# A two-layer transformer block on one core: the second attention's local products with its exponentials as moving columns

## Chip, cores and metric

One core of one Trainium2 chip runs the whole program in one launch, in float32. The time is device microseconds (us), from 3 executions of the kernel. The engines are TensorE (PE, with its weight loads as PEld), VectorE (DVE), ScalarE (ACT), GpSimd (POOL) and SyncE (SP), each with its own instruction stream in a fixed order; they wait for one another by semaphores.

## What is computed

Eight sequences of 512 tokens and 128 features go through two layers. Each layer is an attention (a recurrence in the first, the one below in the second) and a mixture of eight experts of which each token takes two; both with layer norm and modulation around them. The change touches the second attention and the last sum.

```python
# second attention, per sequence x (512 x 128), 16 heads of 8
w = x.reshape(nW=8, 64, 16, 8)                       # windows of 64 tokens
attn = softmax(einsum('nqhd,nkhd->nhqk', w, w) * scale)
local = einsum('nhqk,nkhd->nqhd', attn, w).reshape(512, 128)
comp = conv1d(x, conv_w, stride=4)[:64] + conv_b      # 64 compressed keys
gt = concat([comp, global_memory])                    # 128 keys
glob = softmax(x . gt * scale) . gt                   # 16 heads
mix = sigmoid(concat([local, glob]) @ gate_w + gate_b)
y = (mix * local + (1 - mix) * glob) @ out_w + out_b
# last line of the second layer, y1 and y2 the token's two experts' weighted rows
out = x + gb * (y1 + y2)
```

## The kernel before

The program has four stages: the recurrent attention with the shared expert (0 to 386 us of the trace), the first experts (to 514 us), the second attention (to 1040 us), the second experts (to 1297 us); and then a last sum with loads and stores.

**The second attention** works on eight sequences of 512 tokens in ten steps, `step(i)` for i = -2 to 7, followed by `tail(7)`. Each engine has its own `step`, a list of calls written out by hand, and these lists are the order of the work. In step i each engine does parts of several sequences: f = i+2 (first norm, its sums and transposes), a = i+1 (compressed keys, maxima of the global scores), i itself (exponentials and products), b = i-1 (end of the local part, gate, output, residual), c = i-2 (second norm, modulation), d = i-3 (router, ranks, placing, scatter to the experts' rows in DRAM).

Scores come in six units, each of four PSUM banks (0 to 3) of 128 x 512: four for the global part (heads r of each of four groups g) and two for the local part (`score_local`, `again_local`, l = 0 and 1, four windows each). Every unit's scores are computed twice. In the first pass (`score_global` L2137, `score_local` L2149) DVE takes maxima (`max_global` L1036, `max_local` L1043); they are turned by TensorE (`max_T_global` L2159, `max_T_local` L2167) and negated by ACT. In the second pass (`again_global` L2185 with `less_global` L2194; `again_local` L2213 and L2209) the negated maxima are added, and ACT takes the exponentials (`exps`, L1702 and L1704) into `expT`, two buffers of four rows of 512. A bank can be filled again when the DVE has its maxima or ACT its exponentials (`bank_free` and the waits on c_exp).

**Global products** (`attend_global`, L2224): values of 128 keys x 32 columns are the stationary operand, exponentials move as 512 columns, and the four groups g write four different bands of 32 partitions. The sums stand in banks 6 (heads 0, 1) and 7 (heads 2, 3); ACT (`global_sums`) and DVE (`take_global`, L1058, L1059) take the lower and the upper half of each 32 partitions. `norm_global` inverts the sums (L1049), shuffles and multiplies.

**Local products** (`attend_local`, L2247): the exponentials of one pair of heads are the stationary operand (128 keys x 128), written by `exps` in a permuted order (`expT_l`), and 34 columns of values move: for each of the two windows in a tile 16 values and a one, whose column gives the sum. There are four calls in a step, (l, t) = (0,0), (0,1), (1,0) and, in the following step, (1,1); each has 8 products. The output has queries as partitions. `norm_local` (L1069, L1073) inverts 16 sums and multiplies two halves, per call. `turn_out` (L2261) turns the result back by 4 products, twice a step, and ACT's `mixed_T` (L1712) writes it into `lgT`, in two pieces of two.

After it come `gate` (L2277, L2278), `gate_tanh`, `difference` (POOL, L1371), `mix`, `out` (L1800), `residual` (L1089 and the norm's sums L615, L619), POOL's `ln_scale` and `normalise` (L1202, L1223), `modulate` (L1098, L1100), `h2_T`, `route` (L1805), `router`, `rank` (L1812, L1813), `place`, and POOL's `scatter` (L1234: 8 indirect DMAs a sequence). In `tail` stand what is left of sequence 5 (router, place, scatter), of 6 and of 7, with products that only keep TensorE busy (L1790).

**The last sum.** SP waits until the experts' rows are in DRAM (`y`), loads them, 512 KB a sequence (L599, packets of 1 KB), and stores the outputs (L602). DVE does for each sequence three operations on 128 x 512 (L820, L822, L824): y1 + y2, times gb, plus x.

A matmul or transposition of float32 stands in the trace as two instructions, each with its own weight load; the program order has one.

## Time and profile before

| | us |
|---|---|
| median of 3 runs | 1323.47 (1320.85 to 1325.7) |
| the profiled execution, its own time | 1323.05 |
| its span, first to last instruction | 1321.2 |
| mean granted clock of TensorE over the span | 0.921 of full speed |
| TensorE busy (matmul) | 1157.1, 88% |
| TensorE busy (weight loads) | 816.0, 62% |
| DVE busy | 820.8, 62% |
| POOL busy | 605.6, 46% |
| ACT busy | 497.1, 38% |
| chain that ended last: PE, issue, DVE, DMA, POOL | 58%, 11%, 9%, 8%, 7% |

The page's busy times are unions over overlapping instructions, and a matmul that waits inside a group can be counted as busy, since ends are modelled: for what a group takes, the distance from its start to the next group's start is read. "Granted clock" is 1.00 at 2.4 GHz and 0.50 at 1.2 GHz.

### The profile page before, as it was taken

What the parts mean: (1) busy time and instruction counts of PE and PEld (TensorE: products, weight loads), DVE (VectorE), ACT (ScalarE), POOL (GpSimd) and SP (SyncE); (2) the same over time, 40 slices, a digit from 0 to 9 for tenths busy, and PEclk for the clock granted to TensorE, in tenths of its full rate; (3) what the DMA queues carried; (4) which work ended last, traced back from release to release, by engine and by line L of the source; (5) the groups of instructions that cost most, each with busy time, mean ns of one, the idle gap of its engine ahead of it and who ended that gap; (6) DMA issues with size and microseconds to landing.
All of it is one profiled execution on the core that took longest, in us unless ns stands there. A gap on an engine that the chain in (4) does not pass through costs nothing.

```text
span 1321.2 us, 23979 instructions
## 1 busy us (share of the span) xinstructions
PE 1157.1 (88%) x8027; PEld 816.0 (62%) x8027; DVE 820.8 (62%) x2275; ACT 497.1 (38%) x1147; POOL 605.6 (46%) x706
## 2 busy tenths in 40 slices
PE   6868869867788889899999999999998899999990
PEld 3545546555358886346556465475554599999990
DVE  4678868887334444445457687766646366666665
ACT  3324434433314442142434444424331145444440
POOL 1556858887525554512224546532246233333330
PEclk9788989998889999998889999969899899999996
DMA  4976697673134522100101012000011341111106
GB/s 135 258 185 160 165 260 176 155 164 80 35 76 115 153 80 69 60 23 24 47 10 57 26 49 73 25 23 18 22 39 41 76 118 42 38 46 37 44 20 198
DMA packets 96530, 113.07 MB, mean 86 GB/s; under 512 B 11225, under 2 KB 81177, under 8 KB 93833
## 3 DMA queue, kind: packets, MB, share of 16 engines
q1 hardware_dynamic: 87512, 93.17, 27.1%
q0 software_dynamic: 8640, 17.84, 4.2%
q8 instruction: 66, 1.08, 0.3%
q10 hardware_dynamic: 256, 0.53, 0.2%
q14 instruction: 56, 0.45, 0.1%
HBM read 81.06 MB, written 32.04 MB: 86 GB/s over the span
## 4 chain that ended last, share of the span: by engine, by line
PE 58%; issue 11%; DVE 9%; DMA 8%; POOL 7%; ACT 3%; SPq 2%; DVEq 0%; ACTq 0%; POOLq 0%
PE bank L2027 8%; PE bank L2038 8%; PE bank L2247 5%; PE bank L2185 4%; PE bank L2137 4%; PE bank L2054 3%; PE bank L2194 3%; PE bank L2149 3%; PE bank L2224 3%; PE bank L2213 2%; POOL slots L1234 2%; DMA mrow<-mods 2%; DMA region<-vrdram 2%; POOL region L1270 2%; PE bank L2209 2%
## 5 line engine op out<-in xcount | busy, mean ns | idle before, releaser
L2027 PE MATMUL bank<-rows,wup 128*128 128x128 f32 x1136 | 154.7, 280 | 17.4 <-DVE wup L763 14.1
L1234 POOL DMA_INDIRECT slots<-pay,slot x128 | 130.0, 1016 | 83.4 <-issue 71.6
L1249 POOL DMA_INDIRECT y<-region,xin x78 | 83.9, 1075 | 154.0 <-ACT region L1614 140.7
L2027 PEld LDWEIGHTS bank<-rows,wup 128*128 128x128 f32 x1136 | 141.0, 195 | 21.3 <-DVE rows L751 10.4
L2038 PE MATMUL bank<-rows,wse 128*128 128x128 f32 x1136 | 141.9, 278 | 2.7 <-DVE wse L768 2.7
L2038 PEld LDWEIGHTS bank<-rows,wse 128*128 128x128 f32 x1136 | 132.2, 192 | 9.1 <-issue 7.9
L1036 DVE TENSOR_REDUCE rows<-bank 128x4 f32<-128x512 f32 x128 | 79.5, 684 | 92.6 <-PE bank L2137 86.7
L1249 POOL DMA_INDIRECT y<-hh,region x64 | 69.2, 1082 | 92.9 <-ACT hh L1614 81.9
L1702 ACT ACTIVATE w0uv<-bank 128x512 f32<-128x512 f32 x128 | 66.1, 602 | 90.5 <-PE bank L2194 90.4
L756 DVE SCALAR_TENSOR_TENSOR rows<-bank,bcol,rows 128x128 f32<-128x128 f32 x142 | 43.4, 346 | 90.8 <-ACT rows L1603 90.5
L1790 PE MATMUL bank<-consts 128*128 128x512 f32 x192 | 92.2, 627 | 0.0
L1270 POOL TENSOR_TENSOR region<-region 128x512 f32<-128x512 f32 x64 | 83.4, 1317 | 18.5 <-DVE region L917 17.5
L751 DVE TENSOR_TENSOR rows<-region,bank 128x256 f32<-128x256 f32 x71 | 29.9, 421 | 85.7 <-ACT region L1593 66.7
L1878 PE MATMUL bank<-consts,region 128*128 128x128 f32 x512 | 75.3, 302 | 5.9 <-POOL region L1270 5.7
L2247 PEld LDWEIGHTS bank<-region,w0uv 128*128 128x128 f32 x512 | 72.6, 225 | 11.3 <-issue 10.9
L1878 PEld LDWEIGHTS bank<-consts,region 128*128 128x128 f32 x512 | 70.1, 214 | 12.9 <-POOL region L1270 7.7
L2247 PE MATMUL bank<-region,w0uv 128*128 128x34 f32 x512 | 74.4, 307 | 0.0
L1043 DVE TENSOR_REDUCE wam<-bank 128x8 f32<-128x512 f32 x64 | 39.7, 683 | 39.5 <-PE bank L2149 39.5
L1790 PEld LDWEIGHTS bank<-consts 128*128 128x128 f32 x192 | 36.6, 199 | 41.4 <-issue 41.1
L1704 ACT ACTIVATE w0uv<-bank 128x512 f32<-128x512 f32 x64 | 33.0, 602 | 73.6 <-PE bank L2209 73.6
L915 DVE TENSOR_TENSOR bank<-bank,region 128x512 f32<-128x512 f32 x64 | 44.7, 698 | 25.0 <-DMA region<-vrdram 23.3
L2194 PE MATMUL bank<-rows,pick_g 32*128 32x512 f32 x256 | 53.6, 652 | 0.0
(334 smaller groups left out, 2405.3 us busy)
## 6 DMA issues: line engine op xcount, KB each, us to landing
region<-vrdram SPq DMA_DIRECT2D x16, 1024.0 KB
region<-vrdram SPq DMA_DIRECT2D x32, 512.0 KB, 7.7
xin<-slots SPq DMA_DIRECT2D x78, 65.0 KB
region<-slots SPq DMA_DIRECT2D x64, 65.0 KB
wgl<-in_wgl SPq DMA_DIRECT2D x8, 512.0 KB
rows<-y SPq DMA_DIRECT2D x8, 512.0 KB, 4.3
wgl<-y SPq DMA_DIRECT2D x8, 512.0 KB, 6.5
xres<-x SPq DMA_DIRECT2D x12, 256.0 KB
```

Of the source, the lines that this page charges most:

```text
L1036: V.tensor_reduce(maxg[:, t, g * QD:g * QD + HG], bank[g].rearrange("p (h k) -> p h k", h=HG), axis=AX, op=ALU.max).then_inc(S["c_mx"], 1)
L1234: p.indirect_dma_start(io["slots"], bass.IndirectOffsetOnAxis(ap=slot_of(l, b)[:, k, t:t + 1], axis=0), pay_of(l, b)[:, k, t, :], None).th ...
L1249: p.indirect_dma_start(io["y"], bass.IndirectOffsetOnAxis(ap=xins[par][:, h, k, P + 1:P + 2].bitcast(U32), axis=0), bYs[par][:, h, k, :], ...
L1270: G_.tensor_tensor(rrow[:, j, :], vrow[:, j, :], rrow[:, j, :], ALU.mult).then_inc(S["a_pr"], 1)
L1702: A.activation(expT[k % 2][:, g, :], bank[g], ACT.Exp, scale=SCALE).then_inc(S["c_exp"], 1)
L1790: M(out, ident, consts[:, 0:T], start=True, stop=True)
L1878: ins = M(bank[7][:, tile(t)], rrow[:, j, tile(t)], center, start=(j == 0 and t == 0), stop=(j == DH - 1 and t == NT - 1), skip_group_chec ...
L2027: ins = M(bank_up(l, n)[:, tile(j)], wup[:, n % 3, tile(j)], bxT[:, q % 2, tile(k)], start=True, stop=True)
L2038: ins = M(bank_second(n)[:, tile(j)], wse[:, n % 2, c, tile(j)], bZ[:, n % 4, c, :], start=c == 0, stop=c == FC - 1)
L2137: M(bank[g], xTs[p][heads(g), tile(t)], gmk[p][heads(g), :, :], start=True, stop=True).then_inc(S["c_S"], 1)
L2194: M(bank[g], pick_g[heads(g), r, :], negmax[heads(g), :], start=False, stop=True).then_inc(S["c_E"], 1)
L2247: ins = M(bank[UNIT_BANK[l][t]][:, o:o + 2 * (2 * DH + 1)], expT_l[l][:, t, h, :, :].rearrange("p k q -> p (k q)"), values_l[:, 2 * l + t, ...
```

## The change

1. `attend_local(b, l)` has two calls a step instead of four. The values are now stationary (`values_l`, 128 keys x 32 columns for a pair of heads, block-diagonal over the two windows of a tile, so that half is zero), and the exponentials move, 128 columns for each of 16 products, into bank 6. Four more products with 0/1 weights (`ones_l`) and 512 moving columns give the sums, in bank 7. The four groups g write four bands of 32 partitions.
2. `exps` writes all six units in the same plain order.
3. ACT and DVE take half of each bank (`take_local`, new in both), into `num_l` and `den_l`; DVE inverts `den_l` whole (`invert_local`, 128 x 512) and multiplies once (`norm_local`, 128 x 512). The old `norm_local`, four per step, is gone.
4. `turn` (4 products, 0/1 weights `select`, 256 moving columns each) replaces two `turn_out`; `mixed_T` is one activation instead of four. `local_values` has 2 activations instead of 4.
5. The lists of steps are in another order (below).
6. In the last step router, ranks and placing of sequence 5 are done ahead of the tail. In the tail ACT normalises (`norm_last`) instead of POOL, DVE does `difference`, and there are 13 calls of `keep_busy` products instead of 23 (before `experts`).
7. The last sum: for sequences 2 to 7 TensorE adds y1 and y2 by two products with the identity (`f_s`), DVE does two operations instead of three. x, y and out are laid out so that a partition holds four neighbouring tokens (packets of 4 KB and 2 KB instead of 1 KB and 512 B), and four of the eight loads of y are issued by ACT instead of SP.
8. DVE's preparation ahead of the attention makes `ones_l`, `select`, `kmask`, `wmask` (41 steps instead of 34).

```diff
-            def attend_local(b, l, t):
...
-                for h in range(H // 2):
-                    o = h * 2 * (2 * DH + 1)
-                    ins = M(bank[UNIT_BANK[l][t]][:, o:o + 2 * (2 * DH + 1)], expT_l[l][:, t, h, :, :].rearrange("p k q -> p (k q)"),
-                            values_l[:, 2 * l + t, h, :], start=True, stop=True)
+            def attend_local(b, l):
+
                 t_.wait_ge(S["c_exp"], b * UNITS + (HG + l) * NHG + NHG)
                 if l == 0:
                     t_.wait_ge(S["c_va"], b * VA_STEPS + VA_STEPS)
+                    t_.wait_ge(S["c_took"], b * TAKE_STEPS + 2)
                 else:
+                    t_.wait_ge(S["c_took"], taken(b, 0))
+                for t in range(2):
+                    for q in range(2):
+                        for g in range(NHG):
+                            o = slice((2 * t + q) * P, (2 * t + q + 1) * P)
+                            M(bank[6][heads(g), o], values_l[:, 2 * l + t, 2 * g + q, :], expT[l][:, g, o], start=True, stop=True)
+                for g in range(NHG):
+                    ins = M(bank[7][heads(g), :], ones_l[:, :], expT[l][:, g, :], start=True, stop=True)
                 ins.then_inc(S["c_al"], 1)
...
             def max_T_global(b):
                 t_.wait_ge(S["c_mx"], b * UNITS + SG)
                 if b:
-                    t_.wait_ge(S["c_nl"], normed(b - 1, 0, 1))
+                    t_.wait_ge(S["c_took"], taken(b - 1, 1))
...
+            def take_local(b, l):
+
+                v.wait_ge(S["c_take"], taken(b, l))
+                for src, dst in ((bank[6], num_l), (bank[7], den_l)):
+                    half = dst[:, local_cols(l)].rearrange("p (s q) -> p s q", q=WIN)
+                    V.scalar_tensor_tensor(out=half, in0=by_head(src)[:, :, 1, :], scalar=kmask[:, 1:2], in1=half,
+                                           op0=ALU.mult, op1=ALU.add).then_inc(S["c_took"], 1)
...
+            def invert_local(b):
+
+                v.wait_ge(S["c_took"], taken(b, 1))
+                V.reciprocal(den_l, den_l).then_inc(S["c_rec"], 1)
...
+            def turn(b):
...
+                for w in range(2):
+                    for s in range(2):
+                        ins = M(cols_[:, :, w, :], select[:, w, s, :], rows_[:, :, s, :], start=s == 0, stop=s == 1, skip_group_check=True)
                 ins.then_inc(S["c_ntr"], 1)
...
+            keep_busy(6, bank[BANK_X])
+            t_.wait_ge(S["m_yb"], BLOCKS)
+            for b in range(SUMMED, NB):
+                t_.wait_ge(S[y_loaded(b)[0]], y_loaded(b)[1])
+                out = bank[b - SUMMED].rearrange("p (t d) -> p t d", t=NT)
+                for k in range(2):
+                    ins = M(out, ident, yall[:, b, :, k, :], start=k == 0, stop=k == 1)
+                ins.then_inc(S["f_s"], 1)
```

**TensorE, a full step, from the transposition of the global values (`global_values`, L2124, L2208) on.** In these rows L2247 is the old local product, L2261 the old turn; in the new, L2323 and L2325 are `attend_local`, L2341 is `turn`, L2297 and L2293 are `again_local`, L2359 and L2360 `gate`, L2221 the global scores, L2251 `max_T_local`, L2243 `max_T_global`, L2189 the compression. Before:

```order
833 L2124 MATMUL bank<-consts,gtT 128x128
834 L2137 MATMUL bank<-rows,wsh 128x512 x4
835 L1800 MATMUL bank<-owg,w0d 128x128 x4
836 L2247 MATMUL bank<-region,w0uv 128x34 x8
837 L2213 MATMUL bank<-region,hT 64x256 x16
838 L2209 MATMUL bank<-region,pick_l 64x256 x16
839 L2247 MATMUL bank<-region,w0uv 128x34 x8
840 L2137 MATMUL bank<-rows,wsh 128x512 x4
841 L1795 MATMUL bank<-consts,pay 128x128 x4
842 L2247 MATMUL bank<-region,w0uv 128x34 x8
```

The change:

```order
825 L2208 MATMUL bank<-consts,gtT 128x128
826 L2297 MATMUL bank<-region,hT 64x256 x16
827 L2293 MATMUL bank<-region,pick_l 64x256 x16
828 L2359 MATMUL bank<-w0d,gwT 128x512
829 L2360 MATMUL bank<-w0d,gwT 128x512
830 L2221 MATMUL bank<-rows,wsh 128x512 x4
831 L2323 MATMUL bank<-w0uv,region 32x128 x16
832 L2325 MATMUL bank<-w0uv,ones_l 32x512 x4
833 L2297 MATMUL bank<-region,hT 64x256 x16
834 L2293 MATMUL bank<-region,pick_l 64x256 x16
835 L1884 MATMUL bank<-owg,w0d 128x128 x4
836 L2221 MATMUL bank<-rows,wsh 128x512 x4
```

The first `again_local` stood ahead of the transposition; the gate now stands between it and the scores, and `out` behind the second `again_local`.

**DVE, from the first group of global maxima of a step.** L1036 and L1052 are `max_global`, L820 to L619 and L836 to L635 the front's sums and norm, L1081 to L1085 `norm_global`, L1065 and L1066 `take_global`, L1074 `take_local`, L1090 `invert_local`. Before:

```order
889 L1036 TENSOR_REDUCE rows<-bank 128x4 x4
890 L820 TENSOR_TENSOR rows<-rows 128x4x128
891 L822 TENSOR_TENSOR rows<-rows,wam 128x4x128
892 L824 TENSOR_TENSOR wam<-wam,rows 128x512
893 L615 BN_STATS statsf<-wam 128x6 x4
894 L619 BN_AGGR mvf<-statsf 128x2 x4
895 L1036 TENSOR_REDUCE rows<-bank 128x4 x4
```

The change:

```order
883 L1052 TENSOR_REDUCE rows<-bank 128x4 x4
884 L1081 RECIPROCAL hh<-hh 128x512
885 L1083 STREAM_SHUFFLE rows<-hh 128x512
886 L1085 TENSOR_TENSOR w0d<-w0d,rows 128x512
887 L1052 TENSOR_REDUCE rows<-bank 128x4 x4
888 L1065 SCALAR_TENSOR_TENSOR hh<-bank,wmask,hh 128x512
889 L1066 SCALAR_TENSOR_TENSOR rows<-bank,wmask,rows 128x512
```

and at the end of the step:

```order
905 L1052 TENSOR_REDUCE rows<-bank 128x4 x4
906 L1074 SCALAR_TENSOR_TENSOR hh<-bank,kmask,hh 128x256
907 L1074 SCALAR_TENSOR_TENSOR region<-bank,kmask,region 128x256
908 L1041 TENSOR_TENSOR hT<-hT,posT 128x512
909 L1090 RECIPROCAL region<-region 128x512
910 L1059 TENSOR_REDUCE wam<-bank 128x2x4 x4
911 L1095 TENSOR_TENSOR hh<-hh,region 128x512
```

`norm_global` moved from the step's end to a place between the first two groups of maxima, one step later; the two takes of the local sums stand behind the last maxima, ahead of the inversion.


## Rows read from the trace of the kernel before

**Rows 1.** The page: busy time and share of each engine
```profile
PE 1157.1 (88%) x8027; PEld 816.0 (62%) x8027; DVE 820.8 (62%) x2275; ACT 497.1 (38%) x1147; POOL 605.6 (46%) x706
```

**Rows 2.** Windows by attention step; columns: us, busy (x) per engine, PEclk, DMA share, GB/s
```profile
592.33:644.06 51.73, 51.16 (x434) 29.18 (x429) 29.27 (x56) 21.14 (x43) 13.87 (x14) 0.93 0.11 32
644.06:704.18 60.12, 59.55 (x443) 35.51 (x438) 31.91 (x67) 21.14 (x43) 18.29 (x20) 0.80 0.10 29
704.18:755.14 50.96, 50.39 (x458) 28.63 (x454) 38.59 (x106) 22.38 (x46) 24.44 (x25) 0.97 0.16 48
755.14:805.23 50.09, 49.52 (x459) 28.75 (x454) 38.09 (x105) 22.37 (x46) 26.83 (x29) 1.00 0.16 49
805.23:855.31 50.08, 49.51 (x458) 28.74 (x454) 39.02 (x106) 22.38 (x46) 26.83 (x29) 1.00 0.17 49
855.31:916.00 60.69, 60.12 (x458) 36.38 (x454) 34.82 (x94) 22.36 (x46) 24.11 (x26) 0.80 0.07 22
...
929.94:984.40 54.46, 52.10 (x431) 30.45 (x430) 27.96 (x83) 21.06 (x43) 15.99 (x19) 0.87 0.13 34
```

**Rows 3.** Groups by line, 560 to 1010 us: shapes xcount | busy, mean ns | idle before
```profile
L2247 PE MATMUL bank<-region,w0uv 128*128 128x34 f32 x512 | 74.4, 307 | 0.0
L2247 PEld LDWEIGHTS bank<-region,w0uv 128*128 128x128 f32 x512 | 72.6, 225 | 11.3 <-issue 10.9 <-ACT w0uv L1704 0.3
...
L2224 PEld LDWEIGHTS bank<-w0uv,values_g 128*32 128x32 f32 x256 | 5.5, 110 | 25.8 <-issue 24.7 <-ACT w0uv L1702 1.1
```

**Rows 4.** Timeline of PE in a full-clock step; columns: start us, us, engine, line, operation
```profile
770.63 0.66 PE L2159 MATMUL bank<-consts,rows 128*128 128x128 f32 x4
...
774.41 2.33 PE L2149 MATMUL bank<-region,hT 32*64 32x256 f32 x32
776.67 1.97 PE L2247 MATMUL bank<-region,w0uv 128*128 128x34 f32 x16
778.47 1.04 PE L1805 MATMUL bank<-gatec,rows 128*128 128x8 f32 x8
...
781.37 1.07 PE L2224 MATMUL bank<-w0uv,values_g 128*32 128x512 f32 x8
782.37 2.44 PE L2149 MATMUL bank<-region,hT 32*64 32x256 f32 x32
...
801.61 2.61 PE L2213 MATMUL bank<-region,hT 32*64 32x256 f32 x27
...
806.12 2.59 PE L2137 MATMUL bank<-rows,wsh 32*128 32x512 f32 x8 [0.57 <-ACT w0uv L1704]
...
820.71 0.65 PE L2159 MATMUL bank<-consts,rows 128*128 128x128 f32 x4
```

**Rows 5.** DVE: one window, two timeline rows, two groups
```profile
792.89:819.40 26.51, 19.78 (x46) 1.00 0.24 69
...
771.76 3.35 DVE L1049 RECIPROCAL hh<-hh 128x512 f32<-128x512 f32 x1
...
776.91 2.48 DVE L1043 TENSOR_REDUCE wam<-bank 128x8 f32<-128x512 f32 x4 [0.31 <-PE bank L2149]
...
L1073 DVE TENSOR_TENSOR hh<-bank,recl 64x128 f32<-64x128 f32 x64 | 18.5, 289 | 2.1
...
L1058 DVE SCALAR_TENSOR_TENSOR hh<-bank,half_hi,hh 128x512 f32<-128x512 f32 x8 | 6.0, 747 | 1.3 <-ACT rows L1682 0.9 <-issue 0.4
```

**Rows 6.** Timeline of POOL in the attention's tail
```profile
1000.24 1.09 POOL L1234 DMA_INDIRECT slots<-pay,slot  x1 [6.86 <-issue]
...
1011.84 3.14 POOL L1223 TENSOR_SCALAR xh<-x,mv,rstd 128x128 f32<-128x128 f32 x4 [0.21 <-POOL rstd L1202]
...
1027.84 0.96 POOL L1234 DMA_INDIRECT slots<-pay,slot  x1 [2.25 <-DMA slots<-pay,slot]
...
1037.41 0.96 POOL L1234 DMA_INDIRECT slots<-pay,slot  x1 [0.30 <-issue]
```

**Rows 7.** The end: one window of all engines, and DVE's first operation there
```profile
1299.00:1315.00 16.00, 0.00 (x0) 0.00 (x0) 13.24 (x20) 0.00 (x0) 0.00 (x0) 0.50 1.07 342
...
1301.12 0.69 DVE L820 TENSOR_TENSOR wgl<-wgl 128x512 f32<-128x512 f32 x1 [7.81 <-DMA wgl<-y]
```

377 lines of the change are left out of this document (210 added, 167 removed).

## Prediction

> **What bounds the kernel now.** I read the page first: TensorE is busy 88% of the span, DVE 62% [rows 1]. Then windows over the second attention, cut where the same transposition comes round: a step of it takes 50.09 us at full clock, 50.96, 51.73, 60.12 and 60.69 us at lower ones, with TensorE busy all but 0.57 us [rows 2]. That busy share hides waits. In the timeline of a full-clock step 16 products of `again_local` and what belongs to them start at 801.61 with 27 in the first 2.61 us, and the scores at 806.12 take 2.59 us behind 0.57 us of idling, both waiting for another engine; the first local scores take 2.33 us where ACT hands over banks one by one [rows 4]. So the step is TensorE's chain with two handshakes in it: DVE's maxima and ACT's exponentials. DVE is busy 38.1 of 50.09 us [rows 2], and in the stretch from the first to the last global maxima 19.8 of 26.5 us [rows 5]: it has room, but little there. Everything between 592 and 984 us follows this pattern; the tail behind it is POOL's [rows 6], the last sum DVE's behind DMA [rows 7].
>
> **Local products.** Old: 4 groups of 16 instructions a step, each 1.80 us from its start (776.67) to the next group's (778.47) [rows 4], so 7.2 us. New: twice 32 instructions of 128 columns and 8 of 512. The 8 are `attend_global` over again, 1.00 us (781.37 to 782.37) [rows 4]. The 32 stream as many columns as those 8, so 1.0 us if the loads of the weights stay hidden; I take 1.1. Sum 2 x 2.1 = 4.2 us, 3.0 less. Bounds: below, 2 x 1.9; above, loads that are not hidden, priced as a rival. Evidence for hiding: in the old group a pair of load and product takes 1.80/16 = 0.11 us, though one load's row is 0.225 and one product's 0.307 us [rows 3], so they overlap even though each load covers the whole array.
>
> **Turn.** Two groups of 8 instructions become one of 8 with 256 columns: twice about 1.0 us against about 1.9 (half of what the gate's 512 columns would cost for each); nothing gained in sum, and the new place decides.
>
> **Does the 3.0 us reach the step?** Only in part, as what TensorE stops doing was cover. I follow the new order with `max_T_global` as zero, which starts at 770.63 and 820.71 in the old [rows 4].
> (a) Zero to the end of the first local scores: old 776.67 - 770.63 = 6.0 us. The turn is gone from behind the transposition, and the compression takes its place there; but the compression is then missing between `less_global` and the scores, which wait for ACT. 6.1 us, no gain.
> (b) To the second local scores: the old product of 1.80 us is gone, but `again_global` then runs into DVE's maxima of the scores just made, 4 x 0.6 us. Gain 0.9 us.
> (c) The turn stands where `again_global` waits for the next maxima anyway: free.
> (d) From the first global maxima to the next zero the DVE sets the pace. Old busy time there 19.8 us [rows 5]; out goes one `norm_local` (two products of 0.289 us and a short reciprocal that I take as long as one, 0.87 us [rows 5]); in come `norm_global`, 4.8 us (771.76 to 776.60, that is 776.91 less 0.31) [rows 5], and four takes of 256 columns at 0.4 us, half of the 0.747 us for 512 [rows 5], 1.6 us. Sum 25.3; with small gaps and short waits for scores (I take 1.4, the old order has 6.7) 26.7, and 0.1 to the transposition. Old: 820.71 - 792.89 = 27.8 us. Gain 1.0 us.
> So a full-clock period of 48.2 to 48.9 us; I take 48.3, 1.8 less than 50.09. What is late next is DVE: its inversion of 3.35 us for the local sums lies beside the next step's start, where it has idle time, and the maxima of the last scores start about 1 us after these are there. DVE's total rises by 2.2 us a step (3.35 + 0.7 + 1.6 against 4 x 0.87), to about 40.5 of 48.3.
> For five full steps 9 us, and 0.5 for the ramp: **9.5 us**.
>
> ACT's own part falls a little (activations of `local_values` and `mixed_T`) and rises by four of `take_local`; at 22.4 of 50 us busy [rows 2] I cost both at nothing. If ACT were late, the take of the last sums would delay `max_T_global` at 1 us for 1 us. The DMAs of the steps are unchanged; POOL's `difference` moves behind 8 scatters but is needed only at `mix`, some 8 us later. DVE's 7 further steps of preparation lie ahead of a wait of 6 us for a load: nothing.
>
> **The clock.** Against 50.09 the five steps of rows 2 (with one more at 50.08) and their like lose 1.6 + 10.0 + 0.9 + 0 + 10.6 = 23 us, all where the granted clock falls to 0.50, the lower of its two levels, after the stretch from 800 to 808 us of the pattern with its two handshakes [rows 2, 4]. There the new order puts the gate and the dense products into the gap before the scores, but it adds a wait of about 1 us before `max_T_global`. I take half as lost as before: **11 us**, with 0 and 23 as bounds. TensorE does 3 us less in a period; with DVE setting the pace a low clock costs less too.
>
> **Last step and tail.** From 929.94 to the last scatter's end at 1038.37 are 108.4 us [rows 2, 6]. POOL bounds the old tail: the scatter of sequence 5 starts at 1000.24, then POOL's norm ends at 1015.0, scatter 6 follows, then a wait of 2.25 us for landing, then scatter 7 from 1027.84 [rows 6]. New, from the same zero: the step without next scores 43 us (54.5 before, of which 0.13 x 54.5 = 7 us are clock [rows 2], the rest three pairs of filler products and waits); DVE's take, residual, `norm_global` 4.8, take, inversion 3.4, product, turn, gate, `mix`, router, residual and placing of sequence 6, about 25 us, to 68; eight scatters at 1.27 us (10.2, as 1027.84 to 1038.37 has 10.5), the landing's 2.3, eight more, to 91.5. With 4 us for waits and clock 95.5, so **13 us**; bounds 6 and 17. POOL's 3.14 us for a norm [rows 6] lies on ACT, and scatter 5 ahead.
>
> **Last sum.** DVE's first operation is at 1301.12, then 24 of 0.73 us; DMA moves 342 GB/s at full share for 16 us [rows 7]. New: DVE 2 x 3 + 6 x 2 = 18 operations, 4.4 us less. But TensorE's two products cost 4 x 0.43 = 1.7 us for a sequence, more than DVE's 1.45, and twice that when cold; the granted clock there is 0.50 [rows 7]. With sequence 2 loaded at about 1304.6 (three of its pairs' 1 MB at 350 GB/s from 1299), the chain ends 10.4 + 1.6 + 2.7 us later at 1319.3 warm, 1321.8 with one and a half sequences cold; old 1321.2. I take 0, bounds 2 less and 2 more (a gain from larger packets inside them).
>
> **Sum.** 1323.05 - 9.5 - 11 - 13 - 0 = 1289.5; the profiled execution is 0.4 us below the median. Forecast **1290 us**.
>
> **Rivals.**
> 1. Clock as before (0.20): the handshakes stay, the gate only moves the dip. 1290 + 11 = 1301. For it: the new wait at `max_T_global`.
> 2. Clock nearly full (0.14): 1290 - 11 = 1279. For it: three steps of the same pattern have no deep dip [rows 2].
> 3. DVE takes all of the steps' gain (0.10): the stretch in (d) is not 26.7 but 28.5 us, since 25.3 us of work allow few waits. Then 9.5 is gone, and of the clock's 11 most: 1309 to 1318.
> 4. Weight loads not hidden (0.06), slower: each of the 32 loads of 128 x 32 adds its 0.11 us [rows 3], 3.5 us, and a product 0.03: a call takes 5.4 instead of 2.1 us. The one before the last scores has 0.7 us of slack, the other lies right before `max_T_global`. Period 48.3 + 2 x 3.3 - 0.7 = 54.2, or 4.1 above the old; seven of them 29 us more, the last step 6.6: 1323 + 29 + 6.6 - 13 - 11 = 1335. It is slower from 4.5 us a call (7 x (2x - 0.7) + 2x = 33.5 at x = 2.4). Against it: the pairs of 0.11 us above. The Trainium skill, TensorE: Matmul & The Clock Gate, Part 3, says that a weight load overlaps a product in flight only when it targets other row groups; here every load takes all 128 rows, so by that rule these 32 would not be hidden. The old local products, whose loads also take all 128 rows, speak against it.
> 5. Clock worse (0.04): a 10 us dip in every one of seven steps, for 47 us more than now: 1323 + 47 - 22.5 = 1347.
>
> My forecast (1283 to 1297) has 0.46. A measurement of this kernel tells 0.3%, 4 us, from no change. Faster: 0.46 + 0.20 + 0.14 and most of rival 3, 0.87; within 0.3% 0.03; slower 0.10. The range reaches over rivals 1 and 2 and most of 3, 1268 to 1317, and leaves out 4 and 5.
>
> **What would show it.** The distance between two `max_T_global` near 48.3 us; the local groups 2.1 us a call; DVE almost without idling from the first global maxima to the last take; `again_local` still waiting for maxima, scores behind it no longer for ACT; two instead of three norms between 1000 us and the end of the scatters, and the scatter of sequence 5 inside the last step; the last sum ending on TensorE's products. The forecast is wrong if the local groups take over 3 us, if `max_T_global` waits more than 2 us, or if the tail still shows three sequences' scatters in a row.

## The result, and the profile after

The changed kernel takes 1318.41 us in the median of 20 runs (1314.18 to 1324.3), the kernel before 1324.57 us in 20 runs (1318.27 to 1344.26). The ratio is 0.9959, 95% interval 0.9942 to 0.9975: 5.4 us faster where I had forecast 33, and outside my range. The profiled execution of the changed kernel took 1323.83 us with a span of 1322.0. It lies above its median, so the trace is read for where time sits, and the total is taken from the ratio. Every ratio here compares fast executions alone, while the medians of the kernel before that are given by call include its slower ones, so the two can differ by some tenths of a per cent.

The spans of the two profiled executions in four parts, cut at `max_T_global(0)`, `max_T_global(7)` and the first operation of TensorE for the second experts (1045.43 and 1047.27 us):

| | before | after |
|---|---|---|
| start to `max_T_global(0)` | 557.0 | 560.6 |
| seven steps, `max_T_global(0)` to `(7)` | 374.4 | 379.4 |
| last step and tail | 114.1 | 107.3 |
| experts and last sum | 275.8 | 274.7 |

The page of the changed kernel, busy times (before: [rows 1]):
```profile
PE 1151.1 (87%) x8101; PEld 782.1 (59%) x8101; DVE 839.1 (63%) x2229; ACT 504.6 (38%) x1147; POOL 599.5 (45%) x701
```
Windows by step, cut at the same transposition as [rows 2]; columns: us, busy (x) of PE, PEld, DVE, ACT, POOL, then PEclk, DMA share, GB/s:
```profile
600.49:651.47 50.98, 46.68 (x438) 23.97 (x434) 30.15 (x49) 21.05 (x41) 13.41 (x14) 0.94 0.10 29
651.47:706.55 55.08, 52.52 (x449) 25.98 (x445) 35.13 (x62) 21.61 (x42) 18.37 (x20) 0.84 0.12 35
706.55:759.63 53.08, 51.20 (x465) 27.38 (x462) 40.06 (x98) 22.84 (x45) 24.99 (x27) 0.88 0.15 44
759.63:812.03 52.40, 50.52 (x466) 26.90 (x462) 40.80 (x99) 22.84 (x45) 27.45 (x29) 0.93 0.16 47
812.03:867.03 55.00, 53.12 (x465) 27.15 (x461) 42.16 (x100) 22.84 (x45) 29.25 (x30) 0.87 0.15 46
867.03:920.24 53.21, 51.18 (x466) 27.36 (x462) 40.23 (x97) 22.84 (x45) 25.22 (x28) 0.88 0.10 28
```
Before, two of these six steps lost 10 us each and four were near 50 us [rows 2]. After, none is at full clock throughout: the granted clock of the six is 0.84 to 0.94. Inside one step (windows of PE: us, PE busy, PEclk, DMA share, GB/s):
```profile
831.63:835.27 3.64, 2.75 (x20) 1.00 0.27 78
835.27:838.67 3.40, 3.40 (x40) 1.00 0.34 101
838.67:848.32 9.65, 9.65 (x57) 0.51 0.00 0
```
PE's timeline at that place, and one group of local products before it:
```profile
818.99 1.08 PE L2323 MATMUL bank<-w0uv,region 128*32 128x128 f32 x32
819.89 1.04 PE L2325 MATMUL bank<-w0uv,ones_l 128*32 128x512 f32 x8
820.86 1.86 PE L2297 MATMUL bank<-region,hT 32*64 32x256 f32 x27
...
823.73 1.16 PE L1884 MATMUL bank<-owg,w0d 128*128 128x128 f32 x8
...
831.63 0.63 PE L2243 MATMUL bank<-consts,rows 128*128 128x128 f32 x4 [0.30 <-DVE region L1074]
...
835.27 2.48 PE L2233 MATMUL bank<-region,wsh 32*64 32x256 f32 x32 [0.89 <-ACT w0uv L1783]
837.68 1.06 PE L1889 MATMUL bank<-gatec,rows 128*128 128x8 f32 x8
838.67 3.01 PE L2269 MATMUL bank<-wsh,rows 32*128 32x512 f32 x6
...
844.17 1.94 PE L2308 MATMUL bank<-w0uv,values_g 128*32 128x512 f32 x8
```
The local products are as cheap as I said: 1.87 us a call (818.99 to 820.86). What follows `max_T_global` is the trouble. TensorE idles 0.30 us before it and 0.89 us before the first local scores (L2233). Then come eight products of 8 columns (`route`, L1889), and `again_global(i, p, 1)` (L2269) waits inside its group for DVE's maxima. The clock is at half from 838.9 to 849.1 us. Here stood, before, `turn_out` and a local product of 1.8 us [rows 4].

DVE in the stretch that I had called its pace:
```profile
803.31 2.48 DVE L1052 TENSOR_REDUCE rows<-bank 128x4 f32<-128x512 f32 x4 [1.76 <-PE bank L2221]
...
811.14 2.48 DVE L1052 TENSOR_REDUCE rows<-bank 128x4 f32<-128x512 f32 x4 [0.60 <-issue]
814.37 0.75 DVE L1065 SCALAR_TENSOR_TENSOR hh<-bank,wmask,hh 128x512 f32<-128x512 f32 x1 [0.75 <-ACT rows L1749]
...
830.61 0.48 DVE L1074 SCALAR_TENSOR_TENSOR hh<-bank,kmask,hh 128x256 f32<-128x256 f32 x1 [0.67 <-ACT region L1757]
```
From 803.31 to the last take's end at 831.49 are 28.2 us, where I had 26.7 and the old order 27.8.

The tail, PE and then POOL (answering to [rows 6]):
```profile
988.42 1.35 PE L2323 MATMUL bank<-w0uv,region 128*32 128x128 f32 x32 [3.06 <-DVE region L1074]
...
996.02 5.33 PE L1874 MATMUL bank<-consts 128*128 128x512 f32 x8 [4.54 <-DVE region L1074]
```
```profile
1017.02 1.08 POOL L1289 DMA_INDIRECT slots<-pay,slot  x1 [2.42 <-issue]
...
1030.62 0.96 POOL L1289 DMA_INDIRECT slots<-pay,slot  x1 [3.67 <-DMA slots<-pay,slot]
...
1039.88 0.96 POOL L1289 DMA_INDIRECT slots<-pay,slot  x1 [0.30 <-issue]
```
From `max_T_global(7)` at 939.96 to the last scatter's end at 1040.84 are 100.9 us, before 107.0 (931.35 to 1038.37). Only two sequences' scatters are left behind each other, as planned.

The end, a window and the first operations of DVE and TensorE (answering to [rows 7]):
```profile
1299.00:1315.00 16.00, 9.88 (x18) 4.39 (x19) 8.57 (x13) 0.00 (x0) 0.00 (x0) 0.79 0.84 324
```
```profile
1302.52 0.69 DVE L836 TENSOR_TENSOR wgl<-wgl 128x512 f32<-128x512 f32 x1 [8.68 <-DMA wgl<-y]
...
1305.12 12.93 PE L2475 MATMUL bank<-wgl,consts 128*128 128x512 f32 x24 [6.57 <-DMA wgl<-y]
```
TensorE's 24 instructions end at 1318.05, and only one multiplication and one addition of DVE lie behind them: the chain that I had described, ending within a microsecond of the old one.

### The profile page after: what moved, and what is told of

It is laid out like the page before. It is cut to its first block, busy times and chain, and to the rows that moved or that the text cites. A ratio compares the mean times of both kernels' runs of the same rounds, so it can differ in the third digit from the quotient of the medians.

```text
span 1322.0 us, 24049 instructions
## 1 busy us (share of the span) xinstructions
PE 1151.1 (87%) x8101; PEld 782.1 (59%) x8101; DVE 839.1 (63%) x2229; ACT 504.6 (38%) x1147; POOL 599.5 (45%) x701
## 4 chain that ended last, share of the span: by engine, by line
PE 58%; DVE 13%; issue 9%; DMA 8%; POOL 6%; ACT 4%; SPq 2%; DVEq 1%; another core or an unknown queue 0%; ACTq 0%; POOLq 0%
PE bank L2111 8%; PE bank L2122 8%; PE bank L2221 5%; PE bank L2269 4%; PE bank L2138 3%; PE bank L2233 3%; PE bank L2278 3%; PE bank L2308 3%; DMA region<-vrdram 3%; PE bank L2297 2%; DVE region L933 2%; POOL slots L1289 2%; DMA vrdram<-wgl 1%; DVE bank L931 1%; PE bank L1874 1%
## 5 line engine op out<-in xcount | busy, mean ns | idle before, releaser
L2111 PE MATMUL bank<-rows,wup 128*128 128x128 f32 x1136 | 156.3, 282 | 17.0 <-DVE wup L779 15.3
L1052 DVE TENSOR_REDUCE rows<-bank 128x4 f32<-128x512 f32 x128 | 79.4, 683 | 53.7 <-PE bank L2221 52.2
L1874 PE MATMUL bank<-consts 128*128 128x512 f32 x178 | 88.7, 647 | 4.5 <-DVE region L1074 4.5
L1325 POOL TENSOR_TENSOR region<-region 128x512 f32<-128x512 f32 x64 | 82.4, 1301 | 19.9 <-DVE region L933 18.9
L767 DVE TENSOR_TENSOR rows<-region,bank 128x256 f32<-128x256 f32 x71 | 29.8, 420 | 87.6 <-ACT region L1662 65.1
L1962 PEld LDWEIGHTS bank<-consts,region 128*128 128x128 f32 x512 | 68.8, 210 | 11.6 <-POOL region L1325 7.4
L1874 PEld LDWEIGHTS bank<-consts 128*128 128x128 f32 x178 | 35.4, 207 | 47.0 <-issue 40.7
L2278 PE MATMUL bank<-rows,pick_g 32*128 32x512 f32 x256 | 62.1, 714 | 0.7 <-ACT rows L1768 0.7
L1933 PE MATMUL bank<-rows,wam 128*128 128x512 f32 x80 | 45.6, 653 | 8.0 <-ACT rows L1531 3.5
L1666 ACT ACTIVATE region<-bank,bcol 128x128 f32<-128x128 f32 x142 | 44.6, 364 | 18.8 <-PE bank L2122 18.2
L1662 ACT ACTIVATE region<-bank 128x256 f32<-128x256 f32 x71 | 27.2, 384 | 59.5 <-PE bank L2111 44.7
```

Source lines behind the costliest of these rows:

```text
L1052: V.tensor_reduce(maxg[:, t, g * QD:g * QD + HG], bank[g].rearrange("p (h k) -> p h k", h=HG), axis=AX, op=ALU.max).then_inc(S["c_mx"], 1)
L1325: G_.tensor_tensor(rrow[:, j, :], vrow[:, j, :], rrow[:, j, :], ALU.mult).then_inc(S["a_pr"], 1)
L1874: M(out, ident, consts[:, 0:T], start=True, stop=True)
L1962: ins = M(bank[7][:, tile(t)], rrow[:, j, tile(t)], center, start=(j == 0 and t == 0), stop=(j == DH - 1 and t == NT - 1), skip_group_chec ...
L2111: ins = M(bank_up(l, n)[:, tile(j)], wup[:, n % 3, tile(j)], bxT[:, q % 2, tile(k)], start=True, stop=True)
L2278: M(bank[g], pick_g[heads(g), r, :], negmax[heads(g), :], start=False, stop=True).then_inc(S["c_E"], 1)
```

## Experiments

18 runs of 15 kernels: one is the changed kernel itself, three repeat a kernel of this table (e1_again is e1, g1 is f3, g2 is b1). Two numbers of each trace are used throughout: the **seven steps** (start of `max_T_global(0)` to start of `max_T_global(7)`) and the **clock loss**, the sum of (1 - granted clock) x 5 us over the 103 windows of 5 us from 530 to 1045 us (before 43.5, after 63.7). The tail is `max_T_global(7)` to the last scatter's end. In calls 1, 4 and 5 the attention ends some 40 us earlier, so that these windows also hold the start of the second experts. Rows of one call ran on one chip.

| call | kernel | ratio to before (95%) | median / profiled, us | seven steps | clock loss | tail |
|---|---|---|---|---|---|---|
| - | before | 1 | 1323.47 / 1323.05 | 374.4 | 43.5 | 107.0 |
| - | after | 0.9959 (0.9942-0.9975) | 1318.41 / 1323.83 | 379.4 | 63.7 | 100.9 |
| 1 | e1_fill_scores | 0.9806 (0.9727-0.9885) | 1273.38 / 1274.49 | 364.5 | 30.8 | 93.9 |
| 1 | e2_fill_again | 0.9920 (0.9885-0.9954) | 1286.73 / 1275.16 | 364.4 | 31.4 | 95.9 |
| 1 | e3_fill_both | 0.9792 (0.9717-0.9868) | 1271.16 / 1276.80 | 364.6 | 31.9 | 93.8 |
| 1 | e4_norm_early | 1.0033 (0.9999-1.0066) | 1300.97 / 1302.84 | 381.2 | 56.5 | 99.4 |
| 2 | a2_after | 0.9918 (0.9886-0.9949) | 1317.42 / 1318.03 | 377.0 | 63.4 | 100.6 |
| 2 | b1_fill_before | 0.9867 (0.9812-0.9921) | 1311.44 / 1318.64 | 365.1 | 41.9 | 107.1 |
| 2 | e5_fill_norm | 1.0045 (1.0020-1.0069) | 1332.68 / 1329.37 | 385.8 | 47.8 | 101.7 |
| 2 | e6_sums_dve | 0.9960 (0.9933-0.9988) | 1319.72 / 1321.29 | 376.4 | 58.7 | 101.4 |
| 3 | e1_again | 0.9879 (0.9775-0.9984) | 1301.69 / 1301.36 | 365.9 | 35.4 | 97.3 |
| 3 | e7_cover_back | 0.9962 (0.9926-0.9999) | 1317.98 / 1319.02 | 371.9 | 32.2 | 102.3 |
| 3 | e9_local_twice | 0.9937 (0.9895-0.9979) | 1312.00 / 1309.43 | 367.4 | 30.7 | 99.8 |
| 3 | e8_last_norm | 0.9858 (0.9762-0.9954) | 1302.70 / 1306.10 | 363.3 | 37.5 | 99.7 |
| 4 | f1_one_filler | 0.9928 (0.9901-0.9955) | 1285.91 / 1278.76 | 369.0 | 41.6 | 92.5 |
| 4 | f2_other_gap | 0.9922 (0.9893-0.9951) | 1284.56 / 1286.67 | 374.7 | 53.7 | 95.6 |
| 4 | f3_three_places | 0.9795 (0.9734-0.9857) | 1268.18 / 1264.94 | 355.2 | 15.3 | 93.7 |
| 4 | f4_last_only | 0.9986 (0.9953-1.0020) | 1289.81 / 1285.55 | 377.5 | 54.9 | 93.8 |
| 5 | g1_three_again | 0.9858 (0.9795-0.9921) | 1273.14 / 1273.52 | 359.0 | 22.2 | 93.7 |
| 5 | g2_before_again | 0.9929 (0.9886-0.9972) | 1287.01 / 1288.12 | 361.9 | 31.6 | 102.1 |

Calls differ: the kernel before had 1298.7, 1327.5, 1326.9, 1295.1 and 1298.8 us in them. So times are compared inside a call, and across calls only ratios and the seven steps, and an expectation in absolute time is read as one against after. The seven steps, clock loss and tail are of one execution: those of e2, f1 and f4 were faster than their medians (by 11.6, 7.2 and 4.3 us), that of b1 was slower (by 7.2 us). For them the median and the mean granted clock of the whole kernel over all its runs say more.

The calls differ in a way that the traces show. In the last step of attention, 32 products of `again_local(7, p, 0)` (L2293, L2209) take 1.00 us in every kernel of calls 1, 4 and 5, old order or new, and 4.65 to 6.2 us in every kernel of the others, before and after included. TensorE then stands still between them for nothing that the profile shows. The same kernel, e1 and then e1_again:
```profile
926.85 1.07 PE L2293 MATMUL bank<-region,pick_l 32*64 32x256 f32 x32
```
```profile
950.21 0.60 PE L2293 MATMUL bank<-region,pick_l 32*64 32x256 f32 x5
...
953.97 1.08 PE L2293 MATMUL bank<-region,pick_l 32*64 32x256 f32 x19 [0.76 <-issue]
```
In e1_again 954.98 - 950.21 = 4.77 us pass to the next group, and its tail is 3.4 us longer (97.3 against 93.9); b1's is 5.0 longer than g2's (107.1 against 102.1). So tails are compared only within calls 1, 4 and 5 or within the others.

**Fillers in the weak stretch (e1, e2, e3, f1, f3, g1).** `keep_busy(n, bank)` issues n products of 128 x 512 that nobody reads; bank 6 is free there. The diff is e3; e1 has the first addition alone (f1 with one filler instead of two), e2 the second alone; in f3 and g1 the second is one filler.
```diff
                 if ok(i):
                     less_global(i, 0)
+                    keep_busy(2, bank[6])
                     score_local(i, p, 0)
                 if ok(d):
                     route(d)
                 if ok(i):
+                    keep_busy(2, bank[6])
                     again_global(i, p, 1)
```


> After, with two filler products (128 x 512, into the free bank 6) in every step between the last product of less_global(i, 0) and the first local scores, where TensorE idles 0.89 us for ACT's exponentials. Theory A (the gaps and thin products after max_T_global make the granted clock fall in every step): the dip of 5 to 8 us behind it is gone or much shorter, the clock's loss between 530 and 1045 us falls from 63.7 us to under 35, 15 us or more faster than after (about 1303). Theory B (DVE's chain from the first global maxima to the last take, 28.2 us, paces the step at either clock): dips shorter, time within 4 us of after's 1318. Theory C (dips come by chance, wherever TensorE is not full): loss of the clock about as before, time within 4 us or slower by the fillers, up to 3 us.

> After, with two filler products between route and again_global(i, p, 1), where TensorE waits for DVE's maxima of the first local scores (the place where the old local product stood). A: if this place starts the dips, 63.7 us of clock loss falls to under 35 and the time to about 1305; if the dip has begun before (at the thin compression and the wait for ACT), the clock falls as now and the two fillers at 1.2 GHz cost 1.8 us in each step that dips, so 1320 to 1330. B: within 4 us of 1318. C: within 4 us, or up to 10 us slower.

> After with both pairs of fillers. A: dips gone in nearly all steps, clock loss under 25 us, period 49.5 to 50.5 us, 1295 to 1303. B: clock loss low as well, but the period stays at DVE's 28.2 us plus 22, so 1310 to 1318. C: as after or up to 8 us slower.

e1: the clock loss halves and the seven steps fall by 12 to 15 us against after (377.0 and 379.4). The ratio is 1.5% below after's first here and 0.8% when repeated (e1_again; there the intervals overlap, and neither call had a plain after in it). So A holds, and C, chance, is out. e2 puts two fillers behind the gap of 0.89 us, just where the old local product stood and for as long. In the profiled execution it does as much as e1 for the seven steps; its median is 13 us above e1's in the same call, and its granted clock over all runs 0.931, where e1 has 0.944 and e4, without fillers, 0.918. So this place gives back about half. e3, with both, is not better than e1, and its clock loss of 31.9 us misses the 25 expected. In full-clock steps of e1 and e3 the period is 50.3 to 50.5 us, not the 48.3 of my prediction: that part of B has to be looked at.

> After with one filler (0.92 us at full clock) instead of two ahead of the first local scores, about what TensorE idles there (0.89 us). If the idle time starts the dips: as e1, seven steps in 364 to 368 us, ratio to before 0.980 to 0.990. If what counts is how full TensorE is over a longer stretch: half of e1's effect, 370 to 373 us, 0.985 to 0.993.

One filler gives a ratio of 0.9928, at the edge of the second expectation. The seven steps of 369.0 us are of the fastest of its eight executions; over all of them the granted clock is 0.9245, hardly above the 0.9215 of f4, which has no filler in these steps. So one filler, as long as the idle time, does not do what two do.

**Is DVE's chain the pace? (e4, e5)**
```diff
-                if ok(b):
-                    norm_global(b, b % 2)
                 if ok(a):
                     max_global(a, 1)
...
                 if ok(i):
                     invert_local(i)
+                if ok(i) and i < LAST:
+                    norm_global(i, i % 2)
```


> After with norm_global of a sequence (4.8 us of DVE) moved from between the first two global maxima to the end of the step before, behind the inversion of the local sums, where DVE idles 3.45 us before the first local maxima. B: DVE's stretch from the first global maxima to the last take falls from 28.2 to 24 us, the first local maxima start 1.3 us later, so 2 to 3 us less in a step: 1300 at full clock as now. A: dips stay where they are, gain 0 to 8 us, since TensorE's own work is 26 us of the stretch. If the later first maxima lengthen the dip: up to 10 us slower.

> After with both the two fillers ahead of the first local scores and norm_global moved to the end of the step before. B adds to A: at a full clock the step is paced by DVE's stretch, so the move is worth 1 to 3 us a step here, 7 to 20 us under the fillers alone (ratio to before 0.967 to 0.975). If the move alone was slower because its first maxima come later and feed the dip: 0.980 to 0.990.

Both are slower than after, at 54 to 55 us a step, and e5's ratio of 1.0045 lies outside both of its expectations. DVE's timeline of e1 at full clock, then of e4:
```profile
766.94 2.48 DVE L1052 TENSOR_REDUCE rows<-bank 128x4 f32<-128x512 f32 x4 [1.77 <-PE bank L2221]
...
774.77 1.89 DVE L1052 TENSOR_REDUCE rows<-bank 128x4 f32<-128x512 f32 x3 [0.59 <-PE bank L2221]
...
794.11 0.48 DVE L1074 SCALAR_TENSOR_TENSOR hh<-bank,kmask,hh 128x256 f32<-128x256 f32 x1 [0.72 <-ACT region L1757]
```
```profile
784.50 2.48 DVE L1052 TENSOR_REDUCE rows<-bank 128x4 f32<-128x512 f32 x4 [1.76 <-PE bank L2221]
...
792.33 2.48 DVE L1052 TENSOR_REDUCE rows<-bank 128x4 f32<-128x512 f32 x4 [5.35 <-PE bank L2221]
...
811.67 0.48 DVE L1074 SCALAR_TENSOR_TENSOR hh<-bank,kmask,hh 128x256 f32<-128x256 f32 x1 [0.71 <-ACT region L1757]
```
From the first global maxima to the next local take are 27.17 us in both (766.94 to 794.11, 784.50 to 811.67). DVE has 4.8 us less to do in e4 and idles 5.35 instead of 0.59 us for the next scores. So DVE does not set this stretch, and B falls. What e4 loses is at the step's start. There `norm_global` now holds up the maxima of the first local scores, 2.1 us later and not the 1.3 that I had worked out (8.4 us into the step, after and e1 6.3), and TensorE waits 1.96 us for them (PE of e4, 9 us into the step):
```profile
767.01 3.01 PE L2269 MATMUL bank<-hT,rows 32*128 32x512 f32 x6 [1.96 <-DVE wam L1059]
```
In e5 the clock falls about 2 us behind this wait (a step from 833.55: wait to 842.7, half clock from 844.4). In e4 it falls in the wait or before it, 4.7 to 7.8 us into the step, so there the wait is not what starts the dip. e5 shows that fillers ahead of the scores don't make up for the move.

**Where did the removed products go? (e7, e9)**
Both are built on e1. e7:
```diff
                 if ok(d):
                     route(d)
                 if ok(i):
+                    keep_busy(4, bank[6])
                     again_global(i, p, 1)
```
e9, in `attend_local`, whose two loops of products stand in the new one:
```diff
+                for _ in range(2 if l == 0 else 1):
...
```


> The kernel of e1_fill_scores once more, as the measure for the three others on this chip: a ratio of 0.973 to 0.989 again; steps at full clock of 49.7 to 50.4 us.

> e1 with four more filler products (about 1.7 us) between route and again_global(i, p, 1), as much as the local product that stood there in before. Theory D (each part of the step ends on a handshake: again_global(i, p, 1) waits for DVE's maxima, which start when the first local scores are there; the removed product had lain in that wait): period unchanged to 0.4 us at most at full clock, time within 3 us of e1. My prediction's step (b), by which 0.9 us of the removed 1.8 reached the path: 0.9 us in each of seven steps, 6 us slower than e1.

> e1 with the 40 products of attend_local(i, 0) issued twice (1.9 us more in every step). D: again_local(i, p, 1) behind it takes 2.8 us for 2.0 us of work because it waits for banks, so 0.8 us are hidden, and score_global(a, p, 3) waits 0.6 us for ACT; 0.5 to 1.1 us a step, 4 to 8 us slower than e1. If TensorE's own work were the path there: 1.9 us a step, 15 us slower.

I had mis-sized the filler. PE's timeline of e7, whose step starts at 772.98:
```profile
779.02 1.06 PE L1889 MATMUL bank<-gatec,rows 128*128 128x8 f32 x8
779.94 3.68 PE L1874 MATMUL bank<-consts 128*128 128x512 f32 x8
783.55 1.14 PE L2269 MATMUL bank<-hT,rows 32*128 32x512 f32 x8
784.51 1.03 PE L2278 MATMUL bank<-rows,pick_g 32*128 32x512 f32 x8
785.48 1.06 PE L2308 MATMUL bank<-w0uv,values_g 128*32 128x512 f32 x8
```
Four fillers are eight instructions and 3.6 us, not 1.7. `attend_global(i, 0)` starts 12.50 us into the step (785.48 - 772.98), where in e1's full-clock steps, without these fillers, it starts at 10.74: 1.8 of the 3.6 us were free, and the step takes 52.2 instead of 50.4 us. Had half of the old product reached the path, as my step (b) says, only 0.9 us would have been free. The slack at this place is thus 1.8 us, just what the old local product took there [rows 4]. That product had cost nothing, so its removal could give nothing. e7 as a whole is 16 us above e1_again in the median, 6.0 of it in the seven steps and 5.0 in the tail. e9 adds about 1.8 us further on (PE of e9):
```profile
805.44 1.08 PE L2324 MATMUL bank<-w0uv,region 128*32 128x128 f32 x32
...
807.19 1.06 PE L2324 MATMUL bank<-w0uv,region 128*32 128x128 f32 x32
...
809.04 1.12 PE L2297 MATMUL bank<-region,hT 32*64 32x256 f32 x32
...
810.95 1.16 PE L1884 MATMUL bank<-owg,w0d 128*128 128x128 f32 x8
```
The `again_local` behind it no longer waits (1.91 us to the next group at 810.95, in after 2.87 from 820.86 to 823.73), and the steps at full clock take 51.3 to 51.4 us, 1.0 more, in the range expected of D; the median is 10 us above e1_again, a little more than expected.

**Which gap? (f2, f3)** f2 has one filler ahead of `score_global(a, p, 1)`, 27 us into the step, and f3 all three places.
```diff
+                if ok(i):
+                    t_.wait_ge(S["c_neg"], (i + 1) * NEG_STEPS)
+                    keep_busy(1, bank[5])
                 if ok(a):
                     score_global(a, a % 2, 1)
```


> After with one filler in the step's other gap instead (0.69 us ahead of score_global(a, p, 1), 27 us into the step), and none ahead of the first local scores. A as I put it (the dips start at the first local scores): seven steps in 375 to 380 us as in after, ratio 0.991 to 0.998. Rival A2 (any filled gap serves the clock, the place doesn't matter): 365 to 371 us, 0.982 to 0.990.

> Two fillers ahead of the first local scores, one ahead of again_global(i, p, 1), one ahead of score_global(a, p, 1). A2: the dips that e1 still had are gone, clock loss under 20 us, seven steps in 353 to 360 us (50.4 us each at full clock), ratio 0.972 to 0.982. A alone: as e1, 364 to 367 us, 0.980 to 0.988. If fillers now cost path time: 51 us a step, over 368 us.

> The kernel of f3_three_places again, more rounds: ratio 0.973 to 0.986 once more, seven steps in 353 to 358 us.

f2's profiled execution stays near after (374.7, loss 53.7). f3 has no dip left in six steps. Its windows from one `max_T_global` to the next:
```profile
686.76:737.12 50.36, 50.05 (x470) 25.26 (x470) 40.97 (x99) 22.87 (x45) 26.88 (x29) 1.00 0.17 49
737.12:787.47 50.35, 50.05 (x469) 25.23 (x470) 40.95 (x99) 22.87 (x45) 26.85 (x29) 1.00 0.17 48
787.47:837.82 50.35, 50.05 (x469) 25.25 (x470) 40.89 (x99) 22.87 (x45) 27.87 (x29) 1.00 0.11 32
```
e3 had four fillers a step at the first two places and kept its dips; with one of them moved to the second gap they are gone. So the second gap matters once the start of the step is filled. Whether one filler is worth more at the start than there is not shown: f1 and f2 have the same median (1285.91 and 1284.56 us) and granted clock (0.9245 and 0.924). f3 and its repetition g1 (359.0, just over the 358 expected; the dip in the first step is longer) have the shortest seven steps of this study; e1's and e3's first ratios (0.9806, 0.9792) are as low as f3's 0.9795.

PE of f3 in the full-clock step from 737.12, to be laid beside the old full-clock step from 770.63 [rows 4]:
```profile
737.12 0.63 PE L2243 MATMUL bank<-consts,rows 128*128 128x128 f32 x4 [0.31 <-DVE region L1074]
...
741.71 1.52 PE L2233 MATMUL bank<-region,hT 32*64 32x256 f32 x32
...
747.86 1.07 PE L2308 MATMUL bank<-w0uv,values_g 128*32 128x512 f32 x8
...
764.78 2.29 PE L2221 MATMUL bank<-rows,wsh 32*128 32x512 f32 x8
...
773.46 1.57 PE L2221 MATMUL bank<-rows,wsh 32*128 32x512 f32 x8
```
The same of before, the one row of it that rows 4 leave out:
```profile
799.25 1.43 PE L2137 MATMUL bank<-rows,wsh 32*128 32x512 f32 x8
```
End of the first local scores: 6.11 us in both (741.71 + 1.52 - 737.12; 774.41 + 2.33 - 770.63). Start of `attend_global(i, 0)`: 10.74 and 10.74 (747.86; 781.37). End of `score_global(a, p, 1)`: 29.95 and 30.05. End of `score_global(a, p, 2)`: 37.91 and 38.08. Two orders with 3 us of product work between them arrive at each of these places within 0.2 us.

**Fillers in the kernel before (b1, g2)**
```diff
                     global_values(a)
+                    if ok(i):
+                        t_.wait_ge(S["c_va"], (i + 1) * VA_STEPS)
+                        keep_busy(1, bank[4])
                     score_global(a, a % 2, 2)
```


> Before with one filler product between global_values and score_global(a, p, 2), where its TensorE idles 0.57 us for ACT, ahead of the place where its two deep dips (12 us each) start. If any filled gap serves the clock (the general form of A, no matter which order): clock loss falls from 43.5 to under 30 us, 10 us or more faster, ratio 0.985 to 0.993, and the new order has no merit of its own beside the fillers. If before's dips come by chance (C): ratio 0.998 to 1.002.

> The kernel of b1_fill_before again, on the same chip as g1. If the change has a merit of its own once the clock is served in both, it is the last step and the tail (7 to 10 us), and this stays 0.5 to 1% above g1: ratio 0.983 to 0.991. If a single filler serves the old order as well as four serve the new: within 0.3% of g1.

The old order gains too: 0.9867 and 0.9929 (b1's clock loss of 41.9 us misses the 30 expected, in the slowest of its four executions; g2's ratio is a little over its range). On one chip g1 is at 1273.14 and g2 at 1287.01 us: the new order with four fillers a step is 1.1% faster than the old with one, 0.7% by the ratios, whose intervals overlap slightly. 8.4 us of that lie in the tail (93.7 against 102.1) and 2.9 in the seven steps. The tails are not quite like for like: g1 has its fillers in the last step too, g2's stands in a part that the last step leaves out. Without added fillers in the last step, in one call, the tail is 6.5 us shorter (a2 100.6, b1 107.1). That is the merit of the change that is shown: the last step and the tail.

**Control, the last sum, the last step (a2, e6, f4, e8).** e6 sets `SUMMED = NB` (all sums on DVE). f4 is e1 with its fillers only where `i == LAST`. e8 is e1 with `norm_global(7)` ahead of `mix(6)`.

> After unchanged, as the measure for its variants on this chip. All theories: 0.9942 to 0.9975 of before, as the first time; clock loss between 530 and 1045 us between 50 and 70 us.

> After with all eight final sums on DVE again (24 operations of 0.73 us), loads as in after. My sum: TensorE's products and DVE's fewer operations cancel, 0 with 2 us either way, so 1316 to 1320 where after is 1318. Rival: the chain is bound by TensorE at 1.2 GHz, then 3 to 5 us faster; or by DVE, then the products are worth 3 to 5 us and this is slower by them.

> After with the two fillers in the last step alone. If my tail term (13 us, of which 6.1 came: from max_T_global(7) to the last scatter's end 107.0 us before, 100.9 after) was short by the clock of the last step: 94 to 97 us as in e1, seven steps 376 to 380 us, ratio 0.988 to 0.994. If by work on POOL or DVE: 100 to 101 us, ratio as after.

> e1 with norm_global(7) ahead of mix(6) in the last step, where DVE idles 2.66 us for ACT, and no longer between the residual and take_local(7, 1). If DVE's row of work from mix(6) to the inversion sets the tail (it has no idle time there, and TensorE waits 3.1 and 4.0 us for it): 2 to 2.7 us faster than e1. If the landing of scatters or POOL sets it: no change.

a2 came out at 0.9918, a little below the first interval. e6 is 2.3 us above a2 in the median, of which 1.6 lie behind the start of the second experts (275.4 against 273.8 us). But the intervals of the ratios overlap, and this last part takes 273.6 to 275.9 us in the kernels that have TensorE's sums, so a gain from them, at most about 2 us, is not shown. f4's tail is 93.8 us as with the fillers everywhere (e1 93.9). Against after's 100.9 some 3.6 us of that are the standstill that its call doesn't have, and some 3.5 are the fillers'; among the calls with the standstill they bring the same, 97.3 (e1_again) against 100.6 (a2). The clock's loss from `max_T_global(7)` to the last scatter falls from 11.9 us (after, a2) to 6.8 (f4, e1, e1_again) with them. f4's ratio of 0.9986 misses its range and doesn't resolve such a gain, and its call had no plain after. e8 gave nothing (0.9858 beside 0.9879, intervals wide; tail 99.7 against 97.3). Its `norm_global` went through at 32.6 us behind `max_T_global(7)`, but `mix(6)` then came 3.6 us later than in e1_again and the second take still waited 4.5 us for ACT. DVE's row of work is not the only thing that sets the tail.

## Why the prediction was wrong

**Right.** The local products (1.87 us against 2.1; rival 4 is out). The Trainium skill, TensorE: Matmul & The Clock Gate, Part 3, in its list of what overlaps, would have had these weight loads stand in the open, since they take all 128 rows, though its paragraph on the mechanism also lets a load run ahead into a background weight buffer. 32 pairs of load and product in 0.90 us (818.99 to 819.89) speak against it. Step (a): 6.1 us predicted, 6.05 measured. The last sum's 0 with 2 either way (the last part 1.1 us shorter in the traces). The signs of the tail and of the total.

**Step (b), "Gain 0.9 us", failed.** The gain was 0: `attend_global(i, 0)` starts at 10.74 us in both orders. I saw that `again_global` would run into DVE's maxima and still booked half of the removed product. e7 measured the slack there at 1.8 us, all of the product.

**Step (d), "the DVE sets the pace", failed.** I added DVE's work to 25.3 us, put 1.4 us of gaps on it and got 26.7; the measured stretch is 28.2. e4 took 4.8 us of DVE's work out and the stretch stayed. That DVE's work does not pace it is shown. What does is read from the waits and not tested by a run of its own: the loop over TensorE, DVE and ACT, that is scores, maxima, product again, exponentials, next scores, with a bank changing hands at each turn. TensorE's work beside this loop is free as long as it fits (e7: 1.8 us; e9: 0.8 of 1.8). A full-clock step therefore takes 50.35 us, 0.26 more than before, and the 9.5 us of the sum were really a loss of about 2. Rival 3 (1309 to 1318 us) gave the total about the right size, but for the wrong reason: it had DVE's work as the pace. That it is so near is luck.

**"The clock: I take half as lost as before, 11 us" failed: none of it came.** Against seven steps at full clock (7 x 50.09 = 350.6; 7 x 50.35 = 352.5) the clock took 24 us before, and 27 after and 25 in a2, not 12. The clock loss itself rose more, in the seven steps from 30.7 to 47.0 us (a2 46.6); part of it now falls where TensorE waits anyway. I had the fact in hand, that what TensorE stops doing was cover, and applied it to waits alone. The removed local product and turn had kept TensorE at work between `max_T_global` and the second group of maxima; without them the clock falls to half in or behind that stretch in nearly every step. Fillers of the old product's length in its old place (e2) brought back about half of what two a little earlier did (e1), so the removed work is part of the cause; what the new place of the compression adds to it was not separated. This is rival 5's pattern, a dip in every step, to which I gave 0.04, but mostly at 1 to 5 us a step, not 10: many short dips replace two long ones. Four fillers a step (3.6 us of products that nobody reads) bring the seven steps to 355.2 us, which is about the 354 that my sum had, by luck: by the clock alone and not by the work that I had counted.

**The tail, 13 us, gave 6.1** to the last scatter (6.8 to the experts), at the low end of its bounds. My sum for it (68 + 10.2 + 2.3 + 10.2) is 90.7 and not the 91.5 that I wrote, which changes little. With fillers in the last step it gives 9.7 (e1_again 97.3 against 107.0). So some 3.5 of the 7 us that are missing are the clock of the last step. The old last step had three fillers of its own (`attend_local` with `b == LAST`), which the new order drops; I had booked their time as gain. The remaining 3 us are not traced to one term; TensorE's waits for DVE of 3.06 and 4.54 us lie there.

In sum: 33 us forecast = 9.5 steps + 11 clock + 13 tail + 0. Measured in the two traces: the seven steps 5.0 us longer, the tail 6.8 shorter, the end 1.1 shorter, the part up to the first step 3.6 longer. Of this part the start of the attention, from the first experts' last product with `wup` on, took 45.6 us before, 47.7 after and 50.8 in b1, whose code is the old up to there, so the difference lies within what one kernel shows.

## What to carry to other kernels

Before booking removed work as gain, lay the two orders side by side at each handshake and ask what the last arrival there is: work between two handshakes counts only beyond its slack, which a doubled or filled-in product measures directly (here 1.8 us of 3.6 were free). On TensorE such work may even be useful, since it can keep the granted clock up; a change that removes it should be tried with fillers in the same place, and both orders compared with fillers. A busy share of one engine near 100% in windows, or a row of another engine's work that nearly fills a stretch, is no proof that either is the pace; take some of its work out and see if the stretch moves.

## What the runs showed of the hardware

Small amounts of product work decide how long the clock is granted in full. Two fillers a step raised the granted clock over the whole kernel from 0.918 (e4, no fillers) to 0.944 in the same call, and by the place alone it differed: 0.944 with both ahead of the first local scores (e1), 0.931 with both behind them (e2). One filler left it at 0.924, at either of two places (f1, f2), and four in three places gave 0.95 (f3). The fall of the clock came in or behind a stretch with small gaps, thin products and hidden waits, not behind one long wait: in after it went to half at 838.9 us, with TensorE's only marked idle times since the step's start 0.30 and 0.89 us.

One kernel's profiled executions in two calls, e1 and e1_again, differ by 27 us with nearly the same seven steps (364.5 and 365.9). Most of it is in the first experts: 106.8 us from their first input transposition to their last output (380.85 to 487.63) against 124.1 (384.40 to 508.49). There DVE waits ahead of L767 for nothing that the profile shows, 20 times for 18.9 us, in e1 3 times for 1.7. So it is in every trace: DVE's waits of this kind in this stage are at most 2.3 us in calls 1, 4 and 5 and at least 15 in the others, which are those with TensorE's standstill in the last step. A particular chip is not the reason, since calls 1 and 2 have the same chip number; the cause stays open. Within a call this stage differs by a few microseconds and the ratios hold, but a number of one trace may be set beside one of another call only for stretches that such standstills leave alone.
